# Transposing the quantised activations by DMA instead of on the tensor engine, with the down product in two PSUM banks

## Chip, cores and metric

The kernel runs on one core of one Trainium2 chip. The metric is the device time of one execution in microseconds (us). The program is launched once and holds the whole computation.

## What is computed

A gated cross-attention block followed by a gated feed-forward block, on 16 sequences of 128 tokens with a width of 256. The attention part computes, for each sequence, `x = x + tanh(g0) * attention(layernorm(x), ctx)` with 16 heads of 16. The feed-forward part is what the change touches; the reference, cut to it:

```python
def act_quant(x):
    scale = 127.0 / jnp.clip(jnp.max(jnp.abs(x), axis=-1, keepdims=True), 1e-05)
    return jnp.clip(jnp.round(x * scale), -128, 127) / scale
...
h = bit_linear(x, w1)                              # 256 -> 1024, quantised x, ternary w1
h = depthwise_conv1d(h.transpose(0, 2, 1), conv_w, conv_b)   # 3 taps along a sequence
h = jax.nn.silu(h.transpose(0, 2, 1))
return bit_linear(h, w2)                           # 1024 -> 256: act_quant(h), ternary w2
...
x = x + jnp.tanh(g_ffn[0]) * ffn(layernorm(x))
```

Each of the 16 sequences of 128 tokens is convolved by itself.

## The kernel before

Each engine has its own instruction list, written out by hand, and semaphores order the lists against each other. Sequence number `v` (0 to 15) is one tile of 128 tokens.

In the first part (up to about 165 us) steps 0 to 15 do the attention of one sequence each, and beside it the first linear product and the convolution of the first 12 sequences. A hidden tile `T` (0 to 31) is 128 hidden channels of four sequences; eight such tiles make one group of four sequences. Tiles 24 to 31, those of the last four sequences, cannot start before the attention of sequence 15 is done.

The second part is the subject here. For each sequence `v` it runs this chain:

- `y_transpose(v)` (TensorE, L633): eight transposes of 128x128 that bring the convolved hidden values `y` back to token rows, into `ps_max` or `ps_score`.
- `silu(v)` (ScalarE, L935): PSUM to `z[v]`, 128x1024.
- `token_scale(v)` (VectorE, L1151 to L1156): the absolute maximum of a token over 1024 values, and its scale and reciprocal.
- `quantise2(v)` (GpSimd, L359): `zq` = rounded integers in fp16, offset by 1536, 128x1024; there are four buffers of it.
- `zq_transpose(v)` (TensorE, L696): eight transposes of 128x128 in fp16 into `ps_zq`.
- `quantised_copy(v)` (ScalarE, L941): PSUM to `zqT`, two buffers.
- `project_down(v)` (TensorE, L707, L709): nine matmuls into the one bank `ps_f`, the ninth taking the offset of 1536 out again.
- `residual2(v)` (VectorE, L1161): scale, add to the residual `xres`, and then SyncE stores the tile (L282).

At the same time the hidden tiles 24 to 31 are worked off, one for each of the first eight sequences of the final loop: `hidden(T)` (TensorE, four matmuls, L554), `middle_tap(T)` (ScalarE, L821), `outer_taps(T)` (VectorE, L1041 and L1044, about 0.75 us each). `remainder(15)` (VectorE, L1059) is the last input of `hidden(24)`. After `outer_taps(31)` the values of the last four sequences are complete, and only then can `y_transpose(12)` to `(15)` run.

The final loops of three engines, which fix the order of work, are in short:

```python
# TensorE, v = 0..15:  project_down(v) (v > 0), zq_transpose(v + 1), hidden(24 + v) (v < 8), y_transpose(OPENED[v])
# ScalarE, v = 0..15:  quantised_copy(v + 1), middle_tap(24 + v) (v < 8), silu(OPENED[v])
# VectorE, v = 0..15:  token_scale(v + 3) (v < 9) or (v + 2) (v = 10..13), residual2(v), outer_taps(23 + v) (v < 9)
# OPENED: v + 4 for v < 8; 9: 12 and 13; 10: 14; 11: 15
```

`quantise2(v)` for `v` of 3 to 11 waits for `outer_taps(20 + v)`, so GpSimd starts it when iteration `v - 3` of the VectorE loop has ended. `project_down(v)` waits for `residual2(v - 1)`, because there is one bank. `hidden(T)` waits for `outer_taps(T - 2)`, whose bank it takes. SyncE has issued all loads by 108 us and then only waits for each `residual2` and stores its tile.

## Time and profile before

| | us |
|---|---|
| median of three runs | 236.86 |
| lowest and highest | 234.13, 237.27 |
| profiled execution, from first to last instruction | 235.2 |
| TensorE matmul busy | 215.8 (92%) |
| VectorE busy | 190.4 (81%) |
| ScalarE busy | 161.9 (69%) |
| GpSimd busy | 122.2 (52%) |

The busy shares are means over the whole span. The chain that ended last (followed back from the last instruction) is 68% TensorE, 21% VectorE and 3% ScalarE. In the second part the lines L1151, L1041, L1044 (VectorE) and L707 (TensorE) have the largest shares of it. A granted TensorE clock of 1.00 is 2.4 GHz, and 0.50 is 1.2 GHz.

### The profile page before, as it was taken

The page shows a single profiled execution, that of the slowest core. Times are in us where ns is not written, and L with a number is a line of the kernel's source. Part 1 is how long each engine was busy: PE and PEld are TensorE (multiplying, and loading weights), DVE is VectorE, ACT ScalarE, POOL GpSimd, SP SyncE. Part 2 cuts the span into 40 slices and gives each one's busy share as a digit, 9 for nine tenths or more (in the row PEclk, how much of TensorE's full clock was granted, in tenths as well). Part 3 has the DMA queues.
Part 4 walks back from the last instruction along what each step waited for, and adds up shares of the span by engine and source line. Part 5 has one row for each costly group of instructions (what it writes and reads, how often), then busy time and mean ns, then how long its engine had stood idle before and what let it go on. Part 6 is the DMA issues. An engine that isn't in the chain of part 4 may idle for free.

```text
span 235.2 us, 6424 instructions
## 1 busy us (share of the span) xinstructions
PE 215.8 (92%) x2439; PEld 180.1 (77%) x2452; DVE 190.4 (81%) x387; ACT 161.9 (69%) x318; POOL 122.2 (52%) x229
## 2 busy tenths in 40 slices
PE   7999999997999999999999999989985699997974
PEld 7887787886878787887878878768783588886963
DVE  4163548789798999999999999999899859999671
ACT  2557768777687888989889788667933356674741
POOL 2421326364365757668677576657567224433470
PEclk9999999999999999999999999999999589999999
DMA  5982011010110101100000000000000000111111
GB/s 168 370 270 67 3 49 38 10 46 3 45 47 3 46 3 45 40 11 22 3 3 3 3 0 3 1 3 0 3 0 0 24 25 22 47 46 45 49 52 60
DMA packets 9488, 9.86 MB, mean 42 GB/s; under 512 B 1010, under 2 KB 9202, under 8 KB 9458
## 3 DMA queue, kind: packets, MB, share of 16 engines
q1 hardware_dynamic: 9458, 9.46, 12.2%
q8 instruction: 19, 0.31, 0.6%
q14 instruction: 11, 0.09, 0.1%
HBM read 7.36 MB, written 2.10 MB: 40 GB/s over the span
## 4 chain that ended last, share of the span: by engine, by line
PE 68%; DVE 21%; issue 5%; ACT 3%; DMA 1%; POOL 1%; SPq 0%; ACTq 0%; DVEq 0%; POOLq 0%
PE ps_score L464 10%; PE ps_proj L430 8%; PE ps_proj L509 6%; PE ps_av L487 6%; PE ps_max L474 6%; PE ps_proj L422 5%; DVE zmax L1151 5%; PE ps_proj L413 4%; PE ps_h L568 4%; PE ps_av L707 4%; DVE y L1041 4%; DVE y L1044 3%; DVE smax L987 3%; PE ps_av L497 2%; PE ps_proj L401 2%
## 5 line engine op out<-in xcount | busy, mean ns | idle before, releaser
L987 DVE TENSOR_REDUCE smax<-ps_max 128x8 f32<-128x1024 f32 x31 | 37.9, 1223 | 13.9 <-PE ps_max L474 10.7
L789 ACT ACTIVATE prob<-ps_score 128x1024 f32<-128x1024 f32 x32 | 32.7, 1023 | 17.8 <-PE ps_score L464 16.9
L464 PE MATMUL ps_score<-Qs,KT 32*128 32x128 f32 x512 | 37.1, 283 | 2.0 <-DVE smax L987 0.8
L464 PEld LDWEIGHTS ps_score<-Qs,KT 32*128 32x128 f32 x512 | 31.3, 186 | 9.3 <-issue 5.0
L474 PE MATMUL ps_max<-KT,QT 32*128 32x256 f32 x248 | 35.1, 400 | 0.0
L359 POOL TENSOR_SCALAR zq<-y,zmax 128x1024 f16<-128x1024 f32 x16 | 17.9, 1119 | 29.1 <-issue 18.1
L1151 DVE TENSOR_REDUCE zmax<-y 128x1 f32<-128x1024 f32 x16 | 19.4, 1214 | 5.3 <-ACT y L935 5.3
L336 POOL TENSOR_SCALAR xn<-xn,qa 128x256 f32<-128x256 f32 x16 | 8.1, 508 | 28.1 <-DVE qa L1027 28.1
L829 ACT ACTIVATE y<-hid,conv 128x512 f32<-128x512 f32 x24 | 18.6, 807 | 4.3 <-DVE hid L1034 3.9
L707 PE MATMUL ps_av<-w2q,zqT 128*128 128x256 f16 x128 | 17.4, 281 | 4.3 <-ACT zqT L941 2.6
L474 PEld LDWEIGHTS ps_max<-KT,QT 32*128 32x128 f32 x248 | 21.1, 184 | 0.1
L1044 DVE SCALAR_TENSOR_TENSOR y<-hid,conv,y 128x508 f32<-128x508 f32 x24 | 19.6, 818 | 0.8
L941 ACT ACTIVATE zqT<-ps_proj 128x512 f32<-128x512 f32 x16 | 9.6, 598 | 15.2 <-PE ps_proj L696 15.2
L430 PE MATMUL ps_proj<-xnT,wq 128*128 128x128 f32 x128 | 18.3, 286 | 0.9 <-ACT xnT L763 0.6
L509 PE MATMUL ps_proj<-wo,attT 128*128 128x256 f32 x64 | 18.1, 405 | 1.1 <-DVE w_mean L1124 1.1
L1041 DVE SCALAR_TENSOR_TENSOR y<-hid,conv,y 128x508 f32<-128x508 f32 x24 | 18.7, 778 | 0.0
L430 PEld LDWEIGHTS ps_proj<-xnT,wq 128*128 128x128 f32 x128 | 15.6, 191 | 3.7 <-ACT xnT L763 3.5
L770 ACT ACTIVATE KT<-ps_proj,shift_row,head_mask 128x256 f32<-128x256 f32 x32 | 16.3, 563 | 2.5 <-PE ps_proj L413 2.5
L707 PEld LDWEIGHTS ps_av<-w2q,zqT 128*128 128x128 f16 x128 | 12.1, 101 | 7.2 <-DVE xres L1161 4.9
L487 PE MATMUL ps_av<-prob,V 128*32 128x128 f32 x512 | 17.3, 276 | 0.1
L350 POOL TENSOR_TENSOR hid<-raw,deq 128x512 f32<-128x512 f32 x10 | 13.1, 1311 | 7.9 <-ACT raw L815 7.9
L487 PEld LDWEIGHTS ps_av<-prob,V 128*32 128x32 f32 x512 | 13.0, 110 | 5.4 <-issue 4.5
(140 smaller groups left out, 551.9 us busy)
## 6 DMA issues: line engine op xcount, KB each, us to landing
cin<-ctxT SPq DMA_DIRECT2D x16, 128.0 KB, 2.1
xres<-x SPq DMA_DIRECT2D x16, 128.0 KB, 2.5
out<-xres SPq DMA_DIRECT2D x16, 128.0 KB, 1.7
w1f<-w1T SPq DMA_DIRECT2D x1, 1024.0 KB, 6.2
w2f<-w2T SPq DMA_DIRECT2D x1, 1024.0 KB, 8.1
wk<-wkT SPq DMA_DIRECT2D x1, 256.0 KB, 2.8
wv<-wvT SPq DMA_DIRECT2D x1, 256.0 KB, 4.4
wq<-wqT SPq DMA_DIRECT2D x1, 256.0 KB, 4.6
```

The costliest lines, as they stand in the source:

```text
L430: mm = pe.matmul(ps_q[:, t * P:(t + 1) * P], wq[:, k * D + t * P:k * D + (t + 1) * P], xnT[:, k * P:(k + 1) * P], start=(k == 0), stop=(k ...
L464: mm = pe.matmul(ps_score[:, i * 512 + j * P:i * 512 + (j + 1) * P], KT[b % 3][rows, j * P:(j + 1) * P], Qs[rows, j * P:(j + 1) * P], star ...
L474: mm = pe.matmul(into[:, i * 512 + t * 2 * P:i * 512 + (t + 1) * 2 * P], QT[n % 2][rows, t * P:(t + 1) * P], KT[n % 3][rows, t * 2 * P:(t ...
L487: mm = pe.matmul(ps_av[g * ROW:(g + 1) * ROW, j * P:(j + 1) * P], V[a % VB][:, h * ROW:(h + 1) * ROW], prob[g // PG][:, (g % PG * GH + j) ...
L509: mm = pe.matmul(ps_o, attT[:, t * P:(t + 1) * P], wo[:, t * D:(t + 1) * D], start=(t == 0), stop=(t == KD - 1))
L707: pe.matmul(ps_f, zqT[v % 2][:, c * P:(c + 1) * P], w2q[:, c * D:(c + 1) * D], start=(c == 0), stop=False)
L789: act.activation(prob[pair][:, :], ps_score[:, :], ACT.Exp, scale=DH ** -0.5).then_inc(exp_done, 1)
L829: act.activation(y_tile(T), by_sequence(hid[T % HB][:, :]), ACT.Identity, bias=conv[:, 4 * c + 3:4 * c + 4], scale=conv[:, 4 * c + 1:4 * c ...
L987: dve.tensor_reduce(dst, first_max(n, pair)[:, :].rearrange("p (g t e k) -> p g t e k", g=PG, t=KD, e=2), AX.X, ALU.max).then_inc(max_done, 1)
L1041: dve.scalar_tensor_tensor(y3[:, :, 1:P], h3[:, :, 0:P - 1], conv[:, 4 * c:4 * c + 1], y3[:, :, 1:P], ALU.mult, ALU.add).then_inc(tap0_don ...
L1044: dve.scalar_tensor_tensor(y3[:, :, 0:P - 1], h3[:, :, 1:P], conv[:, 4 * c + 2:4 * c + 3], y3[:, :, 0:P - 1], ALU.mult, ALU.add).then_inc( ...
L1151: dve.tensor_reduce(m[:, 0:1], z[v], AX.X, ALU.max, apply_absolute_value=True).then_inc(zmax_step, 1)
```

## The change

The eight TensorE transposes and the ScalarE copy of each sequence are dropped. In their place SyncE issues one DMA transpose per sequence, `turn_zq(v)`, which reads `zq` (128x1024 fp16, 256 KB) in SBUF and writes the eight transposed 128x128 blocks into `zqT` in SBUF. `zqT` gets four buffers instead of two, each with a semaphore of its own. `zq` and `zqT` now lie in the space of `w2f` and `w1f`, the raw weights, which nothing reads at that time. The first three transposes are issued ahead of the stores; afterwards `turn_zq(v + 3)` follows the store of tile `v` in SyncE's list. `project_down` alternates between `ps_av` and a part of `ps_proj`, and waits for `residual2(v - 2)` instead of `(v - 1)`. On TensorE `project_down(0)` moves behind `int_transpose(15)`, and the filler behind `zq_transpose(0)`, `keep_busy(2)` (four matmul instructions in the trace), goes. On VectorE the calls of `token_scale(12)` to `(15)` are written one iteration earlier but behind `residual2`, which leaves the order of instructions as it was.

```diff
@@ -54,6 +54,7 @@
 OPENED = {v: [v + 4] for v in range(LAST - 4)}
 OPENED.update({LAST - 3: [LAST, LAST + 1], LAST - 2: [LAST + 2], LAST - 1: [LAST + 3]})
 ZQ = 4
+ZT = 4
 
 
 def wait(eng, sem, value):
@@ -148,8 +149,8 @@
         z = [y[:, v * HID:(v + 1) * HID] for v in range(NB)]
         zmax = sb("zmax", [P, 4 * NB])
         zdeq = sb("zdeq", [P, NB])
-        zq = [sb(f"zq{i}", [P, HID], F16) for i in range(ZQ)]
-        zqT = [sb(f"zqT{i}", [P, HID], F16) for i in range(2)]
+        zq = [w2f[:, i * HID // 2:(i + 1) * HID // 2].bitcast(F16) for i in range(ZQ)]
+        zqT = [w1f[:, i * HID // 2:(i + 1) * HID // 2].bitcast(F16) for i in range(ZT)]
 
 
         ps_max = ps("ps_max", 1024)
@@ -169,10 +170,9 @@
         ps_setup = ps_h[:, 0:4]
         ps_z = [ps_max, ps_score]
 
-        ps_zq = ps_proj[:, 0:512]
         ps_late = [ps_h, ps_proj[:, 512:1024]]
         ps_w2sum = ps_h[:, 0:D]
-        ps_f = ps_av[:, 0:D]
+        ps_f = [ps_av[:, 0:D], ps_proj[:, 256:512]]
 
         ident_zero, ident_done, const_done = (
             sem("ident_zero"), sem("ident_done"), sem("const_done"))
@@ -207,9 +207,10 @@
         h_ready, raw_done, scaled_gp, scaled_dve, tap1_done, tap0_done, conv_done, z_done = (
             sem("h_ready"), sem("raw_done"), sem("scaled_gp"), sem("scaled_dve"), sem("tap1_done"), sem("tap0_done"),
             sem("conv_done"), sem("z_done"))
-        zT_ready, zmax_step, zs_done, zdeq_done, zq_done, zqT_ready, zqT_done, f_ready, res_done = (
+        zT_ready, zmax_step, zs_done, zdeq_done, zq_done, f_ready, res_done = (
             sem("zT_ready"), sem("zmax_step"), sem("zs_done"), sem("zdeq_done"), sem("zq_done"),
-            sem("zqT_ready"), sem("zqT_done"), sem("f_ready"), sem("res_done"))
+            sem("f_ready"), sem("res_done"))
+        zqT_in = [sem(f"zqT_in{i}") for i in range(ZT)]
         stored = sem("stored")
 
         block = stack.enter_context(nc.Block())
@@ -243,6 +244,9 @@
 
         def loaded(i):
             return 16 * (i // CB + 1)
+
+        def turned(v):
+            return 16 * (v // ZT + 1)
 
         @block.sync
         def _(sp):
@@ -277,9 +281,20 @@
             for i in range(4, NB):
                 load_x(i)
                 load_c(i)
+
+            def turn_zq(v):
+                sp.wait_ge(zq_done, v + 1)
+                wait(sp, f_ready, v - ZT + 1)
+                sp.dma_start_transpose(zqT[v % ZT][:, :].rearrange("p (c n) -> p c n", n=P),
+                                       zq[v % ZQ][:, :]).then_inc(zqT_in[v % ZT], 16)
+
+            for v in range(3):
+                turn_zq(v)
             for v in range(NB):
                 sp.wait_ge(res_done, v + 1)
                 sp.dma_start(out[v * P:(v + 1) * P, :], xres[:, v * D:(v + 1) * D]).then_inc(stored, 16)
+                if v + 3 < NB:
+                    turn_zq(v + 3)
             sp.wait_ge(stored, 16 * NB)
 
         @block.gpsimd
@@ -355,7 +370,8 @@
                 if 0 <= v - 3 <= len(LATE):
 
                     gp.wait_ge(conv_done, FIRST_LATE + v + 1)
-                wait(gp, zqT_ready, v - ZQ + 1)
+                if v >= ZQ:
+                    gp.wait_ge(zqT_in[v % ZT], turned(v - ZQ))
                 gp.tensor_scalar(zq[v % ZQ][:, :], z[v], zmax[:, 4 * v + 2:4 * v + 3], ROUND16,
                                  ALU.mult, ALU.add).then_inc(zq_done, 1)
                 gp.tensor_scalar(zdeq[:, v:v + 1], zmax[:, 4 * v + 1:4 * v + 2], w_deq[:, 0:1], None,
@@ -516,8 +532,6 @@
 
                     pe.wait_ge(v_done, NB)
                     wait(pe, xq_done, 2 * d if d > LAST else 0)
-                    if d == NB - 1:
-                        pe.wait_ge(zqT_done, 1)
                     for k in range(KD):
                         mm = pe.transpose(ps_xsT[:, k * P:(k + 1) * P], xs[:, k * P:(k + 1) * P], ident[:, :])
                     mm.then_inc(xq_ready, 1)
@@ -685,28 +699,16 @@
                 step(s)
             last_step()
 
-            def zq_transpose(v):
-                pe.wait_ge(zq_done, v + 1)
-                wait(pe, zqT_done, v)
-                if v == 0:
-                    pe.wait_ge(xq_done, 2 * (NB - 1))
-                if v == 1:
-                    pe.wait_ge(xq_done, 2 * NB)
-                for c in range(NC_):
-                    mm = pe.transpose(ps_zq.bitcast(F16)[:, c * P:(c + 1) * P],
-                                      zq[v % ZQ][:, c * P:(c + 1) * P], ident_h[:, :])
-                mm.then_inc(zqT_ready, 1)
-
             def project_down(v):
 
                 if v == 0:
                     pe.wait_ge(att_done, NB)
-                wait(pe, res_done, v)
-                pe.wait_ge(zqT_done, v + 1)
+                wait(pe, res_done, v - 1)
+                pe.wait_ge(zqT_in[v % ZT], turned(v))
                 for c in range(NC_):
-                    pe.matmul(ps_f, zqT[v % 2][:, c * P:(c + 1) * P], w2q[:, c * D:(c + 1) * D],
+                    pe.matmul(ps_f[v % 2], zqT[v % ZT][:, c * P:(c + 1) * P], w2q[:, c * D:(c + 1) * D],
                               start=(c == 0), stop=False)
-                pe.matmul(ps_f, shift16[:, :], w2sum[:, :], start=False, stop=True).then_inc(f_ready, 1)
+                pe.matmul(ps_f[v % 2], shift16[:, :], w2sum[:, :], start=False, stop=True).then_inc(f_ready, 1)
 
 
             project_out(NB - 2)
@@ -729,15 +731,9 @@
             int_transpose(NB - 2, 23)
             keep_busy(12, ps_av)
             hidden(23, LAST)
-            zq_transpose(0)
-            keep_busy(2, ps_av)
-            project_down(0)
             int_transpose(NB - 1, 24)
             for v in range(NB):
-                if v > 0:
-                    project_down(v)
-                if v + 1 < NB:
-                    zq_transpose(v + 1)
+                project_down(v)
                 if v in LATE:
                     hidden(LATE[v], NB)
                 for u in OPENED.get(v, ()):
@@ -934,13 +930,6 @@
                 act.wait_ge(zT_ready, v + 1)
                 act.activation(z[v], ps_z[v % 2][:, :], ACT.Silu).then_inc(z_done, 1)
 
-            def quantised_copy(v):
-
-                act.wait_ge(zqT_ready, v + 1)
-                wait(act, f_ready, v - 1)
-                act.activation(zqT[v % 2][:, :].bitcast(F32), ps_zq, ACT.Copy).then_inc(zqT_done, 1)
-
-
             act.activation(scratch[:, :], ones[:, 0:1], ACT.Silu)
             act.wait_ge(w2q_done, PIECES)
             u_copy(NB - 1)
@@ -955,12 +944,9 @@
             int_copy(NB - 2)
             silu(3)
             middle_tap(22)
-            quantised_copy(0)
             int_copy(NB - 1)
             middle_tap(23)
             for v in range(NB):
-                if v + 1 < NB:
-                    quantised_copy(v + 1)
                 if v in LATE:
                     middle_tap(LATE[v])
                 for u in OPENED.get(v, ()):
@@ -1158,7 +1144,7 @@
             def residual2(v):
                 dve.wait_ge(f_ready, v + 1)
                 dve.wait_ge(zdeq_done, v + 1)
-                dve.scalar_tensor_tensor(at(v), ps_f, zdeq[:, v:v + 1], at(v),
+                dve.scalar_tensor_tensor(at(v), ps_f[v % 2], zdeq[:, v:v + 1], at(v),
                                          ALU.mult, ALU.add).then_inc(res_done, 1)
 
             residual1(NB - 2)
@@ -1183,9 +1169,9 @@
             for v in range(NB):
                 if v + 3 < LAST:
                     token_scale(v + 3)
-                if LAST <= v + 2 < NB:
-                    token_scale(v + 2)
                 residual2(v)
+                if LAST <= v + 3 < NB:
+                    token_scale(v + 3)
                 if v <= len(LATE):
                     outer_taps(FIRST_LATE + 3 + v)
```

## Rows read from the trace of the kernel before

**Rows 1.** Spans of the cores: time from first to last instruction, mean granted TensorE clock
```profile
core 0: 235.2 us, clock 0.984
```

**Rows 2.** Chain that ended last, one steady period: start us, us, what
```profile
200.82 1.16 DVE zmax L1151
...
204.20 1.14 DVE zmax L1151
```

**Rows 3.** Timeline of that stretch: start us, us, engine, line, operation, count, wait before
```profile
197.62 0.47 PE L554 MATMUL ps_proj<-xsT_hi,w1r 128*128 128x512 f32 x1
197.63 1.12 POOL L359 TENSOR_SCALAR zq<-y,zmax 128x1024 f16<-128x1024 f32 x1 [2.51 <-issue]
...
198.62 1.04 PE L633 MATMUL ps_score<-ident,y 128*128 128x128 f32 x8
...
199.69 1.02 ACT L935 ACTIVATE y<-ps_score 128x1024 f32<-128x1024 f32 x1
...
200.75 1.22 DVE L1151 TENSOR_REDUCE zmax<-y 128x1 f32<-128x1024 f32 x1
```

**Rows 4.** Windows: busy us (instructions) of PE, PEld, DVE, ACT, POOL; clock, DMA, GB/s
```profile
182.00:184.00 2.00, 0.00 (x0) 0.00 (x0) 1.97 (x4) 0.81 (x1) 1.20 (x2) 0.86 0.00 0
...
188.00:190.00 2.00, 2.00 (x11) 1.57 (x10) 0.00 (x0) 1.07 (x2) 1.17 (x2) 0.50 0.03 4
...
197.39:200.75 3.36, 3.36 (x32) 2.95 (x30) 3.25 (x7) 2.40 (x3) 1.40 (x2) 1.00 0.11 39
```

**Rows 5.** Timeline where the last hidden tiles begin
```profile
183.84 0.42 DVE L1059 TENSOR_TENSOR xsT_lo<-ps_proj,xsT_hi 128x256 fp32r<-128x256 f32 x1
...
184.40 1.01 PE L696 MATMUL ps_proj<-ident_h,zq 128*128 128x128 f16 x8 [3.31 <-DVE xsT_lo L1059]
...
185.18 0.77 PE L554 MATMUL ps_h<-xsT_hi,w1r 128*128 128x512 f32 x1
...
187.77 1.12 POOL L359 TENSOR_SCALAR zq<-y,zmax 128x1024 f16<-128x1024 f32 x1 [4.49 <-DVE y L1044]
```

**Rows 6.** Timeline after the last outer taps, to the last quantisation
```profile
216.89 0.75 DVE L1044 SCALAR_TENSOR_TENSOR y<-ps_proj,conv,y 128x508 f32<-128x508 f32 x1
...
217.70 1.09 PE L633 MATMUL ps_max<-ident,y 128*128 128x128 f32 x8
...
221.58 1.12 POOL L359 TENSOR_SCALAR zq<-y,zmax 128x1024 f16<-128x1024 f32 x1 [2.29 <-DVE zmax L1156]
...
225.91 1.21 DVE L1151 TENSOR_REDUCE zmax<-y 128x1 f32<-128x1024 f32 x1
...
227.59 1.12 POOL L359 TENSOR_SCALAR zq<-y,zmax 128x1024 f16<-128x1024 f32 x1 [0.70 <-DVE zmax L1156]
```

**Rows 7.** Chain that ended last, its end
```profile
230.20 0.46 PE ps_proj L696 x8
230.69 0.61 ACT zqT L941
231.29 0.14 issue
231.43 1.03 PE ps_av L707 x8
232.46 0.12 PE ps_av L709
232.61 0.48 DVE xres L1161
```

**Rows 8.** DMA queue (packets, MB, share of 16 engines) and issues: KB each, median us to landing
```profile
q1 hardware_dynamic: 9458, 9.46, 12.2%
...
out<-xres SPq DMA_DIRECT2D x16, 128.0 KB, 1.7
...
wk<-wkT SPq DMA_DIRECT2D x1, 256.0 KB, 2.8
...
wo<-woT SPq DMA_DIRECT2D x1, 256.0 KB, 8.3
```

## Prediction, made before the changed kernel ran

> **What bounds the kernel now.** I read the spans first [rows 1]: one core, 235.2 us, the clock near full. Then the chain of waits, because the change lies wholly in the last 55 us and the mean busy shares say nothing about that stretch. It has three parts with different limits, and the reader is to see that in the rows.
>
> In the middle, about 194 to 217.6 us, the chain stays on VectorE and repeats: `token_scale` begins at 200.82 and again at 204.20, a period of 3.38 us, and 3.36 in the windows [rows 2, 4]. In such a window VectorE is busy for 3.25 of 3.36 us and TensorE for all of it [rows 4], but TensorE's time holds a wait: `project_down` there follows each `residual2`. Beside VectorE runs a second loop of nearly the same length [rows 3]: the taps end where the period before 200.82 begins, at 200.82 - 3.36 = 197.46; `hidden` starts at 197.62, then `y_transpose`, `silu`, and the next `token_scale` at 200.75. From `hidden` to `token_scale` that is 3.13 us.
>
> At the end, from the last outer taps at 216.89 + 0.75 = 217.64 us [rows 6], there are 235.2 - 217.64 = 17.56 us. The last steps of the chain there are the pattern of each of the last three sequences [rows 7]: eight TensorE transposes, ScalarE copy, issue, `project_down`, `residual2`. Each costs 231.43 - 230.20 = 1.23 us ahead of a product of 231.43 to 232.61 = 1.18 us.
>
> At the start, TensorE does nothing from 182 to 184 us, and the clock falls to 0.50, the 1.2 GHz level, and is still there at 188 to 190 [rows 4]. When the last input of `hidden(24)` is ready at 184.26, TensorE first does `zq_transpose(1)` from 184.40 and begins `hidden(24)` at 185.18 [rows 5].
>
> **What is removed.** At the start, `zq_transpose(1)` no longer stands ahead of `hidden(24)`: 185.18 - 184.40 = 0.78 us earlier [rows 5]. `hidden(24)`, `y_transpose(4)` and `silu(4)` set the next `token_scale`, so this passes on: -0.78 us. I let the clock be as before, since TensorE has even less to do ahead of 184 us (filler, transposes and the early product are gone or done sooner).
>
> In the middle, 0.5 us of transposes on TensorE and 0.6 us of copy on ScalarE go per sequence, but the period is VectorE's own 3.36 us and VectorE executes what it did, in the same order: 0. What hides it is VectorE; if TensorE were the bound instead, about 0.4 us would come off per period, 3 us in all, and I see no wait of VectorE that would allow it.
>
> The second bank lets `project_down(v)` run ahead of `residual2(v - 1)`. In the middle that too is cover and not gain: 0. At the end it would matter only if the transposed integers were there early.
>
> **What is added.** Let L be the time from the end of the quantisation on GpSimd to the start of the product that reads the transposed buffer. Before, L is 1.23 us plus a queue. No DMA transpose is in the trace, so L is bounded from the nearest rows [rows 8]. Below: a plain load of 256 KB, the same size, lands in 2.8 us, and a store of 128 KB in 1.7, so 2.0 us is the lowest I allow. Above: the worst load of 256 KB took 8.3 us, behind others in the queue. Between them I take the packets. The queue moved 9.46 MB in 9458 packets in 12.2% of 16 engines' span: 0.122 x 16 x 235.2 / 9458 = 48.5 ns for a packet of 1 KB. A transpose of 128x128 blocks of 2-byte values breaks 256 KB into 1024 runs of 256 bytes. At 48.5 ns each over 16 engines that is 3.1 us. The store has 128 such packets, 0.4 us, so its fixed part is 1.3 us, and L = 1.3 + 3.1 = 4.4 us. I take this value: short runs are what the operation consists of, so it is nearer to packets than to a plain load.
>
> The Trainium skill (DMA: Bandwidth & Descriptors, section Why a DMA increments its semaphore by 16 and not by 1, the table of cycles with its column for previous generations) counts 262,144 sequencer cycles for 8,192 tiles from SBUF to SBUF, or 32 a tile. For 64 tiles of 16x128 that is 2,048 cycles, and at 1.2 GHz an estimate of 1.7 us of issue; added to the store's 1.7 us, the sum below would have L = 3.4 instead of 4.4 and end at 238 us instead of 240. The trace of before has no row for it.
>
> Where L lies on the path, part by part:
>
> - Middle. `quantise2(v)` ends 197.63 + 1.12 - 197.46 = 1.29 us after the taps that release it [rows 3], at the start of iteration `v - 2`. TensorE is in order: `project_down(v)` now waits for the DMA, and `hidden(24 + v)`, `y_transpose(v + 4)` are queued behind it, and `silu` and `token_scale` of iteration `v + 1` wait for them. From iteration `v - 2` to `v + 1` are three periods, 10.1 us, and the chain is 1.29 + L + 1.15 + 3.13 = 5.57 + L. It is hidden up to L = 4.5 us; beyond, each period grows by (L - 4.5)/3. At 4.4 it costs 0, with hardly any slack.
> - End. Before, `quantise2(12)` ends at 221.58 + 1.12 = 222.70, which is 5.06 us after the taps [rows 6]. Now `project_down(12)` waits L, takes 1.18, and `residual2(12)` starts 6.24 + L after the taps. VectorE is in order too: `token_scale(15)` is queued behind `residual2(12)` (0.4 us later). It takes 227.59 - 225.91 = 1.68 us to its quantisation, which takes 1.12 [rows 6], so the last integers are there at 9.44 + L. Then L again, 1.18, `residual2(15)` 0.48, and 235.2 - 233.09 = 2.11 us for the last store [rows 1, 7]. Sum: 13.2 + 2L against 17.56 before. L counts twice. With L = 4.4 that is 22.0 us, +4.4.
> - Queues passed. SyncE holds store, then transpose, in order: a store behind a transpose waits for the quantisation, which costs nothing, since only the last store is on the path and the last transpose is issued ahead of it. Four transposes in 9 us at 3.1 us each queue slightly: +0.4. GpSimd's new wait, for the transpose four sequences back, has three periods of slack.
> - Clock. Between the last products TensorE idles for over 2 us, as it did when the clock fell at 182 to 184 [rows 4]. At the low clock a matmul of `hidden` takes 0.77 us against 0.47 [rows 3, 5], a factor of 1.6, so the last product costs +0.7.
>
> Sum on the profiled execution: 235.2 - 0.78 + 4.4 + 0.4 + 0.7 = 239.9, say 240 us. The median of the runs lies 1.7 us above the profiled execution, so 242 us.
>
> **Rivals.**
>
> Hidden anyway, not slower: the transposes are as quick as a plain transfer, L = 2.0 to 3.5. For it speaks that the DMA engines are 11% busy in this stretch [rows 4] and that source and target are on the chip. The sum is 235.2 - 0.8 - 4.4 + 2L, so 234 to 237, or 236 to 239 as a median; it breaks even at L = 2.6. Against it are the short runs. The Trainium skill (Advanced Engine Details and Errata, X-Bar Transpose (TRN2)) says that transposing DMAs are as fast as regular ones, at 350 to 400 GB/s: for 256 KB an estimate of 0.7 us and, with the store's 1.3, an L of 2.0. The trace of before has no transposing DMA to set against it.
>
> One at a time: each transpose starts only when the one before has landed. Then they come at L = 4.4 us, more than the period of 3.36, and the DMA queue is the bound. `zq(3)` is ready at 187.77 + 1.12 - 0.78 = 188.1 [rows 5]; 13 transposes of 4.4 are 57 us, then 1.2 + 0.5 + 2.1: 249 us, 251 as a median. A latency of 6 us without that limit gives 240 + 3.2 + 8 x 0.5 = 247, much the same. For it speaks that the queue's issue is one list and that the data part alone, 3.1 us, is near the period.
>
> Block by block: the fixed 1.3 us is paid for each of the eight blocks, 10.4 us in all, 13 of which make 135 us: 327 us. Only a mechanism that treats blocks as separate transfers does this. The Trainium skill (VectorE: DVE Perf Modes, The three transpose paths) has 1309 ns for one 128x128 block by DMA, which eight in a row would make the same 10.4.
>
> Faster: L is at its lowest and TensorE, relieved of the copy loop, keeps its clock at 184 to 190 us. The work of these 5.6 us would take some 3.3: 234 - 2.3 = 232 us. TensorE's idle time there becomes no shorter, which speaks against it.
>
> **How the numbers follow.** Forecast, L of 3.5 to 5 and overlapping transposes: 0.42, median 239 to 243. Hidden anyway 0.20. One at a time, or a longer latency: 0.25. Block by block 0.08. Faster 0.05. The likeliest gives 242. The range of 236 to 260 leaves out some 0.10 below (faster, and the lower part of hidden) and 0.12 above. 2% is about what a measurement of this kernel can tell from no change; it is 4.7 us, or 241.6, which cuts the forecast in half. Slower by over 2%: 0.25 + 0.08 + 0.22 = 0.55. Faster by over 2%, under 232.1: 0.04. Within 2%: 0.41.
>
> **What would show it.** The period of `token_scale` in the middle: 3.36 if L is hidden, 4.4 if one transpose waits for another, over 10 if blocks do. The issue-to-landing time of the transposes gives L itself. The time from the last outer taps to the end should be 22 to 23 us, with TensorE waiting for DMA at L707, and VectorE waiting at `residual2(12)` with `token_scale(15)` behind it. `hidden(24)` should begin at about 184.4. The prediction is wrong if landing takes under 3 us (then no loss) or if the middle's period changes.

## The result, and the profile after

| | before | after |
|---|---|---|
| median of the runs | 236.57 us (234.13 to 237.27, 4 runs) | 238.34 us (237.6 to 239.91, 4 runs) |
| span of the profiled execution | 235.2 us | 236.5 us |

The ratio is 1.0098, with a 95% interval of 1.0055 to 1.014: slower by 1.0%, where 2.2% was forecast. The direction was right, the size was not, and it lies inside the 2% that I had called no measurable change. A few executions were disturbed and took far longer, or longer by some per cent; they are left out of all ratios, and the profile of e6 below, which is of one of them, isn't read.

The span and clock of the core, to be read against [rows 1]:

```profile
core 0: 236.5 us, clock 0.966
```

The page's DMA queue (packets, MB, share of 16 engines) and its issues (KB each where it applies, median us from issue to landing), against [rows 8]:

```profile
q1 hardware_dynamic: 26354, 13.65, 22.7%
...
out<-xres SPq DMA_DIRECT2D x16, 128.0 KB, 2.0
...
w1f<-w2f SPq DMA_TRANSPOSE x16, 2.8
```

Now L can be read in part: a transpose lands 2.8 us after its issue. The 16,896 added packets of some 248 bytes take 23.7 ns each: (22.7% x 236.5 - 12.2% x 235.2) x 16 / 16,896. I had priced each at 48.5 ns, the time of a packet of 1 KB.

The middle, one period of `token_scale`: us, busy us of PE, PEld, DVE, ACT, POOL, then clock, DMA share, GB/s, against [rows 4]. The next period begins after the same 3.36 us:

```profile
199.53:202.89 3.36, 3.02 (x21) 2.46 (x21) 3.25 (x8) 1.80 (x2) 1.40 (x2) 1.00 0.47 118
```

VectorE is as busy as before (3.25 us), while TensorE is down from 3.36 to 3.02 and ScalarE from 2.40 to 1.80. What was taken off these two engines was cover.

The front, same columns, against [rows 4], and from the timeline the first product of `hidden(24)`, against [rows 5]:

```profile
184.00:186.00 2.00, 1.73 (x4) 1.39 (x5) 1.93 (x6) 0.00 (x0) 0.00 (x0) 0.50 0.45 100
...
188.00:190.00 2.00, 2.00 (x12) 1.50 (x10) 0.88 (x1) 1.02 (x1) 1.09 (x2) 0.56 0.05 8
190.00:192.00 2.00, 2.00 (x17) 1.76 (x16) 1.90 (x6) 1.02 (x2) 0.00 (x0) 1.00 1.27 81
```

```profile
184.27 0.77 PE L568 MATMUL ps_h<-xsT_hi,w1r 128*128 128x512 f32 x1 [1.47 <-DVE xsT_lo L1045]
```

`hidden(24)` begins 0.91 us earlier than before, still at the low level of 1.2 GHz. Its last input was there 0.09 us earlier, at 184.17 against 184.26, so 0.82 us are the change's.

The end. Two figures are used from here on: T, the end of the last outer taps (start of the row plus its duration), and the tail, span less T. Before, T is 217.64 [rows 6] and the tail 17.56. After, T is 216.41 and the tail 20.09. The timeline of that stretch, against [rows 6, 7]:

```profile
215.66 0.75 DVE L1030 SCALAR_TENSOR_TENSOR y<-ps_proj,conv,y 128x508 f32<-128x508 f32 x1
...
220.46 1.12 POOL L375 TENSOR_SCALAR w2f<-y,zmax 128x1024 f16<-128x1024 f32 x1 [2.41 <-DVE zmax L1142]
...
224.47 1.03 PE L709 MATMUL ps_av<-w2q,w1f 128*128 128x256 f16 x8 [1.85 <-DMA w1f<-w2f]
...
225.65 0.48 DVE L1147 SCALAR_TENSOR_TENSOR xres<-ps_av,zdeq,xres 128x256 f32<-128x256 f32 x1 [1.45 <-PE ps_av L711]
...
226.05 1.21 DVE L1137 TENSOR_REDUCE zmax<-y 128x1 f32<-128x1024 f32 x1
...
227.74 1.12 POOL L375 TENSOR_SCALAR w2f<-y,zmax 128x1024 f16<-128x1024 f32 x1 [1.96 <-DVE zmax L1142]
```

And the chain that ended last, its end (start us, us, what):

```profile
228.88 2.77 DMA w1f<-w2f
231.65 0.14 issue
231.78 1.87 PE ps_proj L709 x8
233.65 0.23 PE ps_proj L711
233.88 0.03 issue
233.90 0.48 DVE xres L1147
```

The reader sees L twice: from 221.58 to 224.47 (2.89 us, sequence 12) and from 228.86 to 231.78 (2.92 us, sequence 15). Between them stands `residual2(12)` at 225.65, waiting 1.45 us for its product, with `token_scale(15)` behind it at 226.05. The last product takes 1.87 us for its eight matmuls where it took 1.03 [rows 7]. The windows there, columns as above, show TensorE busy for 0.26 us of two, and then the low level:

```profile
230.00:232.00 2.00, 0.26 (x3) 0.19 (x3) 0.48 (x1) 0.00 (x0) 0.00 (x0) 0.68 0.91 240
232.00:234.00 2.00, 1.86 (x9) 1.01 (x7) 0.10 (x1) 0.00 (x0) 0.00 (x0) 0.50 0.07 22
```

From 235.2 to 236.5 the accounts are: T 1.23 us earlier, tail 2.53 us longer. The tail's 2.53 is 13.2 + 2 x 2.92 - 17.56 = 1.48 for L, 0.94 for the slow last product (231.78 to 233.90 against 1.18 us), and 0.1 that is left. This 0.1 is no queueing of the last transposes: it lies ahead of them, between T and the integers of sequence 12 (5.17 us, before 5.06). `project_down(9)` waited so long for its transpose that the transposes of `y` behind it began 0.22 us after T (before 0.06, [rows 6]):

```profile
215.65 1.03 PE L709 MATMUL ps_proj<-w2q,w1f 128*128 128x256 f16 x8 [2.80 <-DMA w1f<-w2f]
216.63 1.04 PE L647 MATMUL ps_max<-ident,y 128*128 128x128 f32 x8
```

T and the tail come from one profiled execution of each kernel, and the one of before had a mean granted clock of 0.984 [rows 1]. Of 62 other executions of before, taken beside the experiments, 12 had 0.984 or 0.985 and spans of 234.7 to 235.3 us, 45 had 0.989 to 0.993 and 233.7 to 234.8 us, and 5 had 1.000 and 232.5 or 232.6 us. So the profiled execution is one of the longer ones, and the 1.23 us at the front are counted from it. The medians differ by 1.77 us; with the tail's 2.53 that leaves an estimated 0.76 us for the front, give or take the 1 us of the interval.

### The profile page after: what moved, and what is told of

It reads as the page before. It is cut to its first block, busy times and chain, and to the rows that moved or that the text cites. A ratio compares the mean times of both kernels' runs of the same rounds, so it can differ in the third digit from the quotient of the medians.

```text
span 236.5 us, 6153 instructions
## 1 busy us (share of the span) xinstructions
PE 211.6 (89%) x2320; PEld 172.2 (73%) x2320; DVE 190.5 (81%) x387; ACT 152.4 (64%) x302; POOL 122.2 (52%) x229
## 3 DMA queue, kind: packets, MB, share of 16 engines
q1 hardware_dynamic: 26354, 13.65, 22.7%
## 4 chain that ended last, share of the span: by engine, by line
PE 62%; DVE 21%; issue 8%; POOL 3%; ACT 2%; DMA 2%; POOLq 1%; SPq 0%; ACTq 0%; DVEq 0%
PE ps_score L480 9%; PE ps_proj L446 8%; PE ps_proj L525 6%; PE ps_av L503 6%; PE ps_max L490 6%; PE ps_proj L438 5%; DVE zmax L1137 5%; PE ps_h L582 4%; PE ps_proj L429 4%; DVE y L1027 4%; DVE y L1030 3%; DVE smax L973 3%; PE ps_av L513 2%; PE ps_proj L417 2%; DVE xres L1147 2%
## 5 line engine op out<-in xcount | busy, mean ns | idle before, releaser
L375 POOL TENSOR_SCALAR w2f<-y,zmax 128x1024 f16<-128x1024 f32 x16 | 17.9, 1118 | 29.4 <-issue 16.9
L429 PE MATMUL ps_proj<-cin,wk 128*128 128x128 f32 x128 | 17.0, 276 | 0.0
L981 DVE SCALAR_TENSOR_TENSOR Qs<-ps_score,max_row,QT 128x256 f32<-128x256 f32 x32 | 13.9, 478 | 3.3 <-PE ps_score L454 3.3
L438 PE MATMUL ps_proj<-wv,cin 128*128 128x256 f32 x64 | 16.5, 381 | 0.0
```

The lines of the kernel that those rows point to most:

```text
L429: mm = pe.matmul(ps_k[:, t * P:(t + 1) * P], wk[:, k * D + t * P:k * D + (t + 1) * P], cin[n % CB][:, k * P:(k + 1) * P], start=(k == 0), ...
L438: mm = pe.matmul(ps_v, cin[n % CB][:, k * P:(k + 1) * P], wv[:, k * D:(k + 1) * D], start=(k == 0), stop=(k == KD - 1))
```

## The experiments

All on one core; each median stands against executions of the kernel before taken beside it (ratio with its 95% interval). T, tail and span are of one profiled execution each.

| run | T | tail | span | median | ratio |
|---|---|---|---|---|---|
| before | 217.64 | 17.56 | 235.2 | 236.57 | |
| after | 216.41 | 20.09 | 236.5 | 238.34 | 1.0098 (1.0055 to 1.014) |
| e1_one_ahead | 216.87 | 25.8 | 242.7 | 243.96 | 1.0344 (1.0294 to 1.0394) |
| e2_two_ahead | 224.49 | 34.0 | 258.5 | 259.56 | 1.1007 (1.0952 to 1.1062) |
| e3_scale15_first | 216.04 | 18.96 | 235.0 | 237.06 | 1.0038 (1.0012 to 1.0064) |
| e4_zq1_behind | 219.65 | 17.55 | 237.2 | 237.58 | 1.0073 (1.004 to 1.0106) |
| e5_two_halves | 216.91 | 23.4 | 240.3 | 242.13, one run | none |
| e6_tail_filler | not read | not read | not read | 238.79 | 1.0085 (1.0049 to 1.0122) |
| e7_last4_tensor | 216.64 | 19.06 | 235.7 | 236.96 | 1.003 (1.0015 to 1.0046) |
| e8_one_bank | 216.60 | 20.0 | 236.6 | 238.88 | 1.0122 (1.0082 to 1.0162) |
| e9_before_filler | 214.86 | 17.64 | 232.5 | 234.44 | 0.9932 (0.9907 to 0.9958) |
| e10_after_filler | 215.07 | 20.03 | 235.1 | 237.47 | 1.0073 (1.0034 to 1.0112) |
| e11_all | 214.42 | 16.18 | 230.6 | 232.75 | 0.9862 (0.979 to 0.9935) |
| e12_no_dma | 215.08 | 15.72 | 230.8 | 232.65 | 0.9847 (0.9822 to 0.9873) |

### Does L stand on the path, and do transposes wait for one another? (e1, e2)

Spare transposes of the same integers into free memory are issued ahead of the real one, one in e1 and two in e2:

```diff
                 wait(sp, f_ready, v - ZT + 1)
+                for j in range(EXTRA):
...
+                    sp.dma_start_transpose(spare(j, v).rearrange("p (c n) -> p c n", n=P),
+                                           zq[v % ZQ][:, :]).then_inc(spare_in[2 * j + v % 2], 16)
                 sp.dma_start_transpose(zqT[v % ZT][:, :].rearrange("p (c n) -> p c n", n=P),
```

> The changed kernel with one spare DMA transpose of the same integers, into the unused space of prob, issued just ahead of each real one. It sets the latency L (end of the quantisation to start of the product, 2.92 us for the last sequence in the changed kernel) on purpose. Theory (L lies twice on the path at the end, 13.2 + 2L after the last outer taps, and is hidden in the middle up to 4.5): an issue takes 1.23 us, so L becomes about 4.2, the period of token_scale stays 3.36, and the span grows by 2 x 1.25 = 2.5 us, from 236.5 to 239.0. Rival one (transposes run one at a time): L becomes 2.92 + 2.8 = 5.7, the period at least 5.6, and the span grows by over 20 us. Rival two (L lies on the path once): +1.3 us.

> The changed kernel with two spare DMA transposes ahead of each real one. Theory: L is about 2.92 + 2 x 1.25 = 5.4 us, past the 4.5 us that the middle hides, so each of some eight periods grows by (5.4 - 4.5)/3 = 0.3 to 3.66 us, and the end by 5.0: span 236.5 + 5.0 + 2.4 = 244 us. SyncE then issues 3 x 1.25 + 0.6 = 4.3 us per sequence, more than the period of 3.36, so a bound by issue would give a period of 4.3 and a span of some 250 us. Rival (one at a time): a period of 8.4 us and a span over 280 us.

Measured: e1 +6.2 us on the span, e2 +22.0. The chain of e1 at its end:

```profile
227.06 1.23 SPq L297
228.29 0.04 issue
228.33 2.83 DMA w1f<-w2f
...
233.00 0.58 SPq L306
...
233.69 1.23 SPq L297
234.92 0.04 issue
234.96 2.85 DMA w1f<-w2f
```

Two things follow. First, the landing stays at 2.83 and 2.85 us although a transpose was issued 1.27 us ahead of it: transposes of one queue overlap, and "one at a time" falls. Second, what is one at a time is the issue on SyncE. A spare, a real transpose and a store take 1.23 + 1.31 + 0.58 us and the gaps, 3.32 us in all; in the middle that hides below the period of 3.36, while at the end, where four sequences come in quick succession, the issues are spaced 3.32 us. So e1 cost more than L alone would; in addition its last two products ran at the low level (1.87 and 1.86 us), where after has one such product. In e2 SyncE's list, 4.68 us for each sequence, is the bound from the middle on. A theory that counted only the landing gave too little for both. e1 therefore doesn't tell whether L counts once or twice at the end; its period of 3.36 us shows that the middle hides the longer L.

### What does the size of the transpose cost? (e5)

```diff
-                sp.dma_start_transpose(zqT[v % ZT][:, :].rearrange("p (c n) -> p c n", n=P),
-                                       zq[v % ZQ][:, :]).then_inc(zqT_in[v % ZT], 16)
+                for h in range(2):
+                    cols = slice(h * HID // 2, (h + 1) * HID // 2)
+                    sp.dma_start_transpose(zqT[v % ZT][:, cols].rearrange("p (c n) -> p c n", n=P),
+                                           zq[v % ZQ][:, cols]).then_inc(zqT_in[v % ZT], 16)
```

> The changed kernel with each transpose split into two of 512 columns. It measures how the price divides into a fixed part and one by the size. A price by runs (1.3 us and 1024 runs at some 1.4 us, which is what the landing time of 2.8 us leaves) gives halves that land in about 2.0 us, with an issue of 0.6 each if the issue goes by size. A price that is mostly fixed gives halves that land in over 2.4 us. Span within 1 us of 236.5.

From the page's issues and the chain that ended last:

```profile
w1f<-w2f SPq DMA_TRANSPOSE x32, 2.4
```

```profile
231.82 1.20 SPq L290
233.02 0.04 issue
233.06 2.42 DMA w1f<-w2f
```

A half is issued in 1.20 us, as a whole is (1.23), and lands in 2.42, against 2.77. So the issue doesn't go by the size. 128 KB more cost 0.35 us; against the 2.84 of e1, where another transpose was in flight too as it is here, they cost 0.42. That is an estimate of 310 to 370 GB/s. The landing of a whole is then roughly 2.0 us that the size doesn't move, and some 0.75 that it does. The Trainium skill (Advanced Engine Details and Errata, X-Bar Transpose (TRN2)) puts transposing DMAs at the speed of regular ones, 350 to 400 GB/s; the 310 to 370 of this pair roughly agree. The Trainium skill's table of sequencer cycles (DMA: Bandwidth & Descriptors, section Why a DMA increments its semaphore by 16 and not by 1) goes by the number of tiles; the issue measured here did not, and was 1.23 us where I had estimated 1.7 from it.

The span of 240.3 us missed what was expected of e5, which was to stay within 1 us of 236.5. Two issues and a store take SyncE 3.2 us for a sequence, so at the end the issues are the bound, as in e1. It is one run; its median is not compared.

### Does L count twice at the end? (e3)

```diff
-                if v + 3 < LAST:
+                if v + 3 < LAST or v + 3 == NB - 1:
                     token_scale(v + 3)
                 residual2(v)
-                if LAST <= v + 3 < NB:
+                if LAST <= v + 3 < NB - 1:
                     token_scale(v + 3)
```

> The changed kernel with token_scale(15) ahead of residual2(12) on VectorE, nothing else. Theory (the last token_scale is queued behind a residual that waits for a DMA transpose, so L counts twice): the last integers come about 1.9 us earlier and the span falls from 236.5 to 234.6 us, with another 0.9 if the shorter idle time of TensorE keeps its clock. Rival (the end is set by TensorE or by the DMA queue, whatever VectorE does first): no change, 236.5.

VectorE, then SyncE, in the timeline of e3:

```profile
223.91 1.22 DVE L1137 TENSOR_REDUCE zmax<-y 128x1 f32<-128x1024 f32 x1
...
225.44 0.48 DVE L1147 SCALAR_TENSOR_TENSOR xres<-ps_av,zdeq,xres 128x256 f32<-128x256 f32 x1
```

```profile
226.74 0.57 SPq L295 DMA_DIRECT2D out<-xres  x1
227.43 1.24 SPq L288 DMA_TRANSPOSE w1f<-w2f  x1
```

The chain that ended last in e3:

```profile
225.45 3.01 DMA w1f<-w2f
...
228.59 1.86 PE ps_av L709 x8
...
230.67 1.58 PE ps_proj L709 x8
```

`token_scale(15)` no longer waits for `residual2(12)`: the last integers are there 10.74 us after T instead of 12.45, which is 1.71 us earlier where 1.9 was expected, so one of the two L is off the path. The tail is only 1.13 us shorter; the other 0.37 us of the span's 1.5 is T, which this edit doesn't touch. The rest is lost in two places. On SyncE the last two transposes stand behind stores: the last integers are there at 226.78, and their transpose is issued at 227.43. On TensorE the last two products both run at the low level (1.86 and 1.78 us), and the chain now goes through both of them, behind the transpose of sequence 14.

### What did the front gain come from? (e4, e9, e10)

e4 is the kernel before with only the order of the change: `zq_transpose(1)` and its copy stand behind `hidden(24)` and `y_transpose(4)`. e9 is the kernel before with 13 filler products ahead of the wait of `hidden(24)`; e10 is the kernel after with fillers there and behind `project_down(0)`.

e4 on TensorE (ScalarE's copies move likewise):

```diff
-                if v + 1 < NB:
+                if 0 < v < NB - 1:
                     zq_transpose(v + 1)
...
                     y_transpose(u)
+                if v == 0:
+                    zq_transpose(1)
```

e9, then e10:

```diff
             int_transpose(NB - 1, 24)
+            keep_busy(13, ps_xT)
```

```diff
+            keep_busy(10, ps_xT)
             int_transpose(NB - 1, 24)
             for v in range(NB):
                 project_down(v)
+                if v == 0:
+                    keep_busy(10, ps_xT)
```

> The kernel before with the TensorE transposes and the ScalarE copy of sequence 1 moved behind hidden(24) and y_transpose(4), nothing else: no DMA transpose. Theory (the front gain of the change is only that these transposes no longer stand ahead of hidden(24)): hidden(24) starts 0.8 us earlier and the last outer taps end 0.8 to 1.2 us earlier, span 235.2 to about 234.2. Rival (the front gain needs TensorE to be relieved of transposes altogether): the taps end less than 0.4 us earlier.

> The kernel before with 13 filler calls (26 matmul instructions, about 2.9 us at full clock) on TensorE behind int_transpose(15), where it idles from 181.1 to 184.4 us and the clock falls. Theory (some of what the change gains at the front is hidden behind the low clock that both kernels have there): hidden(24), y_transpose(4) and the product run at 1.00, token_scale(5) comes 2 to 2.7 us earlier, span 235.2 to about 233 us. Rival (the clock there costs nothing, since VectorE sets the pace): within 0.5 us of 235.2.

> The changed kernel with filler matmuls in the two idle stretches ahead of hidden(24), from 177.7 to 180.2 and from 181.8 to 184.2 us. Theory: the clock is 1.00 at 184 us, token_scale(4) comes at 187.5 where VectorE is ready, and the last outer taps end about 2.0 us earlier than in the changed kernel (216.41), so 214.4; the end takes 20 us as before, span 234.5 us. Rival (filler delays int_transpose(15) or the first product and with them the rest): no gain.

The windows of e4, then one of e9:

```profile
190.00:192.00 2.00, 2.00 (x12) 1.45 (x12) 0.84 (x3) 0.00 (x0) 0.00 (x0) 0.50 0.00 0
192.00:194.00 2.00, 2.00 (x13) 1.72 (x12) 1.88 (x3) 0.60 (x1) 0.00 (x0) 0.69 0.19 66
```

```profile
188.00:190.00 2.00, 2.00 (x18) 1.67 (x16) 1.93 (x5) 1.34 (x2) 1.12 (x2) 1.00 0.00 0
```

In e4 `hidden(24)` began 0.72 us earlier (184.46), as the change of order should give, and T came 2.01 us later. `project_down(1)` waited 0.84 us for the ScalarE copy, and TensorE, with that gap, stayed at the low level to about 193 us. This profile is of one of e4's three longest executions (spans of 237.1 to 237.4 us; the other seven 235.2 to 236.3), so 2.01 is more than e4 usually costs; its ratio says 0.7%. In e9, where TensorE did filler work through the wait, the clock was full through this stretch and T came 2.78 us earlier than before: more than twice what the change gained. The span of e9, 232.5 us, is also that of the five executions of before whose clock stayed at 1.000 without any filler, so it is the clock that gives this gain.

How much of T is the change's and how much the clock's is seen best when T is counted from the moment at which the last input of `hidden(24)` is there. That moment itself differs between executions of kernels whose lists are alike up to there: it lies between 184.12 and 184.73 us in after, e3, e7 and e8, and at 184.83 and 184.18 in e10 and e11.

| kernel | transposes at the front | input there | T | T less input |
|---|---|---|---|---|
| before | TensorE | 184.26 | 217.64 | 33.38 |
| e4 | TensorE, behind `hidden(24)` | 184.36 | 219.65 | 35.29 |
| after | DMA | 184.17 | 216.41 | 32.24 |
| e3 | DMA | 184.38 | 216.04 | 31.66 |
| e7 | DMA | 184.73 | 216.64 | 31.91 |
| e8 | DMA, one bank | 184.12 | 216.60 | 32.48 |
| e9 and e12, with filler | TensorE | 184.20, 184.41 | 214.86, 215.08 | 30.66, 30.67 |
| e10 and e11, with filler | DMA | 184.83, 184.18 | 215.07, 214.42 | 30.24, 30.24 |

With the clock kept, the DMA transposes save 0.42 us, in both pairs. This is just the time that `zq_transpose(1)` takes ahead of `hidden(24)` at the full clock (in e9 from 184.34 to 184.76); at the low clock it takes the 0.78 of [rows 5]. Without filler the four kernels with DMA transposes differ among themselves by 0.8 us (by 0.6 without e8, which has one bank), though their lists are alike up to T. The product behind `y_transpose(4)` begins at 187.82 us in both e3 and after; in e3 its eight matmuls take 1.04 us, in after 1.91, so the low clock ends at a different time in the same front. Of the 1.23 us by which T moved, then, 0.8 us are order, and the other 0.4 us lie within what one execution differs from the next.

### Do the second bank, and filler at the end, matter? (e8, e6)

e8 takes the second bank away, e6 puts filler ahead of the last two products:

```diff
-        ps_f = [ps_av[:, 0:D], ps_proj[:, 256:512]]
+        ps_f = [ps_av[:, 0:D], ps_av[:, 0:D]]
...
-                wait(pe, res_done, v - 1)
+                wait(pe, res_done, v)
```

```diff
+                if v >= NB - 2:
+                    keep_busy(5 if v == NB - 2 else 7, ps_xT)
                 project_down(v)
```

> The changed kernel with the down product back in one PSUM bank, waiting for the residual just before it; the DMA transposes stay. Theory (the second bank is cover in the middle, where VectorE sets the period of 3.36 us): the period stays within 0.05 us, the span within 1 us of 236.5. Rival (the second bank is what lets TensorE keep up once it waits for the DMA): a longer period and a span over 238.

> The changed kernel with filler matmuls on TensorE ahead of the last two products, sized to end before their input lands. Theory (the last product runs at the low clock because TensorE idled for the transposes): the clock stays at 1.00, the last product takes 1.15 us instead of 2.1, and the span falls from 236.5 to 235.6 us. Rival (filler only delays the products): no gain.

e8: 236.6 against 236.5 us, and the same period of 3.36: the second bank is cover. e6 brought no measurable gain (1.0085 against 1.0098); whether the last products kept their clock can't be told from its median, so what the slow last product costs is read from the timeline of after alone.

### Can the end be mended? (e7, e11)

e7 is the kernel after, where the integers of the last four sequences are turned by TensorE ahead of the products, in two banks that are free by then. e11 has this, the order of e3 and the front filler of e10.

```diff
-                if v + 3 < NB:
+                if v + 3 < LAST:
                     turn_zq(v + 3)
...
+                if LAST <= v < NB - 1:
+                    zq_transpose(v + 1)
                 project_down(v)
...
+                act.activation(zqT[v % ZT][:, :].bitcast(F32), ps_late[v % 2][:, :], ACT.Copy).then_inc(zqT_done, 1)
```

> The changed kernel with the last four sequences transposed by TensorE and copied by ScalarE as before, in banks that are free by then; sequences 0 to 11 stay on the DMA queue. Theory (the front gain of 1.2 us is kept, and the loss is wholly the two latencies at the end): the time from the last outer taps to the end is 17 to 17.6 us instead of 20.1, the span 233.8 us, below the 235.2 of the kernel before. Rival (DMA transposes also slow the rest): above 235.

> What the experiments point to: DMA transposes for sequences 0 to 11 where their latency is hidden, TensorE and ScalarE for the last four where it is not, token_scale(15) ahead of residual2(12), and the front filler. Theory: last outer taps at about 214.4 us, and from there 15.5 to 16.5 us (17.56 in the kernel before), span 230 to 231 us, 2% faster than the kernel before. Rival (TensorE idle for over 2 us at project_down(9), which waits for a DMA, lets the clock fall ahead of y_transpose(12), as in the run with the last four on TensorE): another 1 us, 231 to 232.

e7's timeline of TensorE:

```profile
215.43 1.03 PE L722 MATMUL ps_proj<-w2q,w1f 128*128 128x256 f16 x8 [2.34 <-DMA w1f<-w2f]
...
216.69 1.97 PE L648 MATMUL ps_max<-ident,y 128*128 128x128 f32 x8
```

The tail of e7 was 19.06 us, not the 17 to 17.6 expected. `project_down(9)` had waited 2.34 us for its transpose, and the next transposes of `y` ran at the low level (1.97 and 1.78 us; in e8, with T at almost the same time, 1.09 and 1.04). The product behind them began 1.6 us later than in e8, and without that the tail would be 17.5. The wait alone doesn't explain the low clock: e8 waited 2.42 us and after 2.80 at this place, and both kept the full clock behind it. In e11 the wait was 1.00 us, the transposes took 1.09 again, and the tail was 16.18. e11 is faster than both kernels.

### What of e11 was the DMA's doing? (e12)

e12 is the kernel before with e9's filler, e11's order at the end and its free banks, and no DMA transpose at all.

```diff
+                to = ps_late[v % 2][:, :] if v >= LAST else ps_zq
...
+                if LAST <= v < NB - 1:
+                    zq_transpose(v + 1)
                 if v > 0:
                     project_down(v)
-                if v + 1 < NB:
+                if v + 1 < LAST:
                     zq_transpose(v + 1)
...
-                if LAST <= v + 2 < NB:
+                if LAST <= v + 2 < NB - 1:
                     token_scale(v + 2)
+                if v == NB - 4:
+                    token_scale(NB - 1)
```

> The kernel before, with its integer transposes all on TensorE, and three edits of the version that was faster than both: 13 filler products at the front, token_scale(15) ahead of residual2(12), and the last four integer transposes ahead of the last down products, which alternate between two banks. Theory: in that version the gain came from the clock at the front and from the order at the end, and the DMA transposes of the first twelve sequences of the second half added at most 0.5 us. Then the last outer taps end at about 214.9 us, the tail is about 16.2 us and the span about 231.1 us. Rival: the DMA transposes freed TensorE in the middle or at the front and carried the gain: the span is then 232.5 us or more, no better than the kernel before with fillers alone.

The spans of e11 and e12:

```profile
core 0: 230.6 us, clock 0.999
```

```profile
core 0: 230.8 us, clock 1.000
```

The medians are 232.75 and 232.65 us. T is 0.66 us earlier with the DMA transposes, of which 0.23 is an input that was there earlier and 0.43 is the order shown above; the tail is 0.46 us longer: nothing is left. So the 1.4% of e11 and the 1.5% of e12 are the clock at the front (e9 alone 0.7%) and the order and banks at the end (changed together, and not told apart), and need no DMA transpose.

## Why the prediction was right and wrong

**The structure held.** L is hidden in the middle (period 3.36, as said), stands on the path at the end and counts there twice (e3 took one of them off, and the last integers came 1.71 us earlier), through `residual2(12)` ahead of `token_scale(15)` on VectorE. The formula 13.2 + 2L gives 19.0 us with the measured L; with the slow last product it is 20.0, and 20.09 was measured.

**The term that failed: L.** I took 4.4 us, and it was 2.9. The step that failed is "short runs are what the operation consists of": 1024 runs at the 48.5 ns of a packet of 1 KB. The added packets took 23.7 ns each, and e5 shows that the size moves some 0.75 us of a whole landing, not 3.1. The time of a long packet is no price for a short one; it is at most an upper bound, and I used it as the value. The fixed part was too low in turn, 1.3 against some 2.0 us: a transpose has its own, and the store of [rows 8] didn't show it. The two errors in part cancelled. Nor would the right packet price have been enough: at 23.7 ns my sum gives 1.3 + 1.6 = 2.9 us, but that agreement is luck, for a half it gives 2.1, and halves landed in 2.42. Since L counts twice, 2 x 1.48 = 2.96 us of the 3.4 us by which the span was missed (239.9 against 236.5) are this term. Of the two estimates that I had drawn from the Trainium skill, 3.4 (DMA: Bandwidth & Descriptors) and 2.0 (X-Bar Transpose (TRN2)), the measured 2.92 lies between; the second has about the right rate, but its fixed part, the store's 1.3, is too small. The reading of 1309 ns a block (VectorE: DVE Perf Modes, The three transpose paths) as eight in a row falls: eight blocks land together in 2.8 us.

**The front.** I had 0.78 us. The start of `hidden(24)` moved by 0.82 against its input, so this term was right; T moved by 1.23, which is 0.45 us of the miss in the span. I took the clock there as unchanged. In the profiled execution it came back some 0.7 us sooner (TensorE's matmuls are short from about 189.6 us, before from about 190.3; the window of 188 to 190 has 0.56 against 0.50 in [rows 4]), but that moment differs from one execution to the next of the same front, as e3 shows, and the change isn't shown to move it. By the medians the front gained an estimated 0.76 us. e4 shows that the direction was not safe: nearly the same earlier start with one more gap behind it made the kernel 0.7% slower.

**The small terms.** Clock on the last product: 0.7 forecast, 0.94 measured. Queueing of the last transposes: 0.4 forecast, none measured (L is 2.89 us for sequence 12 and 2.92 for sequence 15); what queues is the issue (1.23 us), not 3.1 us of data.

**The rivals.** "Hidden anyway" had the right L (2.0 to 3.5) and by its sum 235.2 - 0.8 - 4.4 + 5.8 = 235.8 us of span; what it lacked was the clock at the last product. The measured 238.34 lies in its upper end as well as near my own lower one. I gave it 0.20, and it deserved most of what "one at a time" (0.25) and "block by block" (0.08) had: both gave each transfer a serial cost for which no row of before spoke. They are excluded by e1's landings and by the unchanged period.

**What stays open.** One landing of after took 4.5 us against a median of 2.8, and `project_down(9)` waited 2.80 us for it; in e7 and e8 the same product waited 2.34 and 2.42 us for landings of 4.1, and in e3, e10 and e11, where the landing took 2.7, only 1.00 us. The profile shows something beside it. In the window of 212 to 213 us of after, a queue that the profile calls an instruction queue carries this (packets, MB, share of 16 engines):

```profile
q8 instruction: 1, 0.02, 6.9%
```

From 188 us on, 61 landings of transposes in after, e3, e7, e8, e10 and e11 can be read singly. 13 of them took over 3 us, and each of these has a packet of an instruction queue (q8 or q14) beside it. The 40 without such a packet took 2.7 or 2.8 us. All 9 with a packet of q8 took 3.3 to 4.5 us, while 8 of those with one of q14 took 2.8. So the late landings go with these packets; that they are caused by them is not shown, since no run moves such a packet on purpose. Open is also why the clock fell behind the wait of e7 and not behind the longer ones of after and e8, and whether filler can keep the clock of the last product.

## What to carry to other kernels

When work moves from an engine to a DMA, the price is a latency, not a throughput: find each place where it stands between a result and the next step, and count how often an in-order engine makes it count on the path. Here the engines that were relieved had been cover in the middle, and at the end 1.23 us of transposes and copy were exchanged for 2.92 us of latency. Before moving work off TensorE, look at its granted clock where it waits: filler in one gap gave 0.7% (e9), and order and free banks at the end as much again (e12 against e9), while the change itself cost 1.0%.

## What the runs showed of the hardware

- A transpose by DMA from SBUF to SBUF takes 1.23 us of the issuing engine's list, for 128 KB as for 256 KB. A store issued right behind it takes 0.58 us of issue, where one that stands by itself takes 0.34; stores land in a median of 2.0 us (1.7 in [rows 8]).
- Landing is 2.8 us for 256 KB and 2.4 for 128 KB, and stays 2.8 with another transpose 1.27 us ahead in the same queue. It was 3.3 to 4.5 us in all 9 cases with a packet of the instruction queue q8 beside it.
- TensorE's waits for these transposes can show in its clock, and don't always: the last product took 1.87 us behind a wait of 1.74 (and so in e8 and e10, behind 1.77 and 1.78), and the transposes of `y` 1.97 us a little after a wait of 2.34 in e7, but 1.04 and 1.09 after waits of 2.80 and 2.42 in after and e8.
- The granted clock of one and the same kernel differs between executions: before had 1.000 in 5 of 62, with spans of 232.5 or 232.6 us, and otherwise 0.984 to 0.993, with 233.7 to 235.3 us.
